# Building a graph aggregation's dense blocks: chunk order, table storage, and where the gathered steps stand

## What is computed

```python
def _graph_conv(x, W, edge_src, edge_dst, edge_weight, n_nodes):
    support = x @ W
    msg = support[edge_src] * edge_weight[:, None]
    return jax.ops.segment_sum(msg, edge_dst, num_segments=n_nodes)
...
h = _graph_conv(features, W1, edge_src, edge_dst, edge_weight, n)
out = _graph_conv(h, W2, edge_src, edge_dst, edge_weight, n)
...
xn = _layernorm(x, axis=-1)
x = x + _L0_gnn_ref(xn, ...) + _L0_mix_ref(xn[None], ...)[0]
x = x + _L0_ffn_ref(_layernorm(x, axis=-1)[None], ...)[0]
```

## Time and profile before

| | us |
|---|---|
| median of the three runs | 3638.55 |
| profiled execution, its own time | 3613.85 |
| its span | 3612.2 |
| TensorE busy, and its share of the span | 2916.3 (81%) |
| layer 1, unit 0 (76.2 to 149.6) | 73.4 |
| layer 1, units 1 to 26 (149.6 to 1512.2) | 1362.6 |
| all that follows, layer 2 first | 2100.0 |

### The profile page before, as it was taken

How to read it: one execution, slowest core, us unless ns; L and a number is a source line. 1 busy time by engine, 2 the same in 40 slices (tenths; PEclk the granted TensorE clock), 3 DMA queues, 4 the chain that set the end, 5 groups by cost and what they waited for, 6 DMA issues and landing times.

```text
span 3612.2 us, 49615 instructions
## 1 busy us (share of the span) xinstructions
PE 2916.3 (81%) x14732; PEld 2068.0 (57%) x14733; DVE 1420.1 (39%) x3945; ACT 1455.2 (40%) x3127; POOL 1844.7 (51%) x1924
## 2 busy tenths in 40 slices
PE   1799999899989999768988888888877648988930
PEld 0466556556656665546655666566546647777830
DVE  7544554554455446322222222222215541111157
ACT  4677776777777777300000000000004423333322
POOL 3555555545555555256666666666643651222235
PEclk9899999999999999979998999999988869999975
DMA  6344434434443443375555555555532334444454
GB/s 217 119 137 142 143 108 142 142 103 143 146 139 114 141 146 131 104 236 173 177 173 167 174 178 177 164 178 176 174 93 88 119 123 131 135 142 131 118 155 125
DMA packets 257759, 525.92 MB, mean 146 GB/s; under 512 B 47793, under 2 KB 144056, under 8 KB 257337
## 3 DMA queue, kind: packets, MB, share of 16 engines
q1 hardware_dynamic: 142492, 263.69, 22.4%
q0 software_dynamic: 84240, 228.40, 21.0%
q10 hardware_dynamic: 30832, 31.42, 2.7%
HBM read 387.33 MB, written 137.44 MB: 145 GB/s over the span
## 4 chain that ended last, share of the span: by engine, by line
PE 52%; issue 12%; DVE 11%; another core or an unknown queue 10%; ACT 6%; DMA 5%; SPq 3%; DVEq 1%; ACTq 1%; POOL 0%; POOLq 0%
PE bank L911 28%; PE bank L899 8%; PE sums L924 5%; DVE pa L1295 4%; DMA pa<-ys_d 4%; PE bank L1134 3%; PE bank L988 2%; PE bank L934 1%; ACT build L709 1%; ACT build L707 1%; PE sums L882 1%; ACT pa L833 1%; PE bank L943 1%; SPq L537 1%
## 5 line engine op out<-in xcount | busy, mean ns | idle before, releaser
L606 POOL DMA_INDIRECT pa<-xn_d,srcs x768 | 739.8, 963 | 667.4 <-PE sums L924 481.6
L606 POOL DMA_INDIRECT pa<-h_d,srcs x768 | 756.1, 985 | 398.2 <-issue 212.6
L911 PE MATMUL bank<-t1s,pa 128*128 128x256 f32 x2646 | 657.6, 398 | 100.0 <-issue 79.8
L899 PE MATMUL bank<-build 128*128 128x343 f32 x1620 | 559.9, 477 | 130.5 <-DVE build L1280 54.7
L1295 DVE TENSOR_TENSOR pa<-bank,pa 128x343 f32 x810 | 417.4, 515 | 603.8 <-ACT pa L714 462.8
L911 PE MATMUL bank<-t0s,pa 128*128 128x256 f32 x2646 | 612.5, 389 | 45.2 <-DVE pa L1295 37.4
L911 PEld LDWEIGHTS bank<-t1s,pa 128*128 128x128 f32 x2646 | 515.8, 199 | 231.5 <-issue 143.2
L911 PEld LDWEIGHTS bank<-t0s,pa 128*128 128x128 f32 x2646 | 504.7, 194 | 155.4 <-issue 86.2
L899 PEld LDWEIGHTS bank<-build 128*128 128x128 f32 x1620 | 279.8, 192 | 376.1 <-issue 298.1
L709 ACT ACTIVATE build<-build,ones 128x343 f32<-128x343 f32 x810 | 471.3, 582 | 26.3
L707 ACT ACTIVATE build<-build,l1tab 128x343 f32<-128x343 f32 x810 | 458.8, 566 | 37.3 <-issue 24.6
(11 more groups left out here) (247 smaller groups left out, 2565.9 us busy)
## 6 DMA issues: line engine op xcount, KB each, us to landing
slab_d<-pa SPq DMA_DIRECT2D x189, 448.0 KB
pa<-slab_d SPq DMA_DIRECT2D x189, 448.0 KB
pa<-in_w ACTq DMA_DIRECT2D x32, 512.0 KB, 4.0
pa<-in_w SPq DMA_DIRECT2D x32, 512.0 KB, 3.7
pa<-ys_d SPq DMA_DIRECT2D x109, 130.0 KB
pa<-eo_d SPq DMA_DIRECT2D x49, 256.0 KB, 3.2
pa<-xn_d,srcs POOLq DMA_INDIRECT x768
pa<-h_d,srcs POOLq DMA_INDIRECT x768
```

The costliest lines, as they stand in the source:

```text
L606: pool.indirect_dma_start(gath[g % RING * QT + j], None, table, bass.IndirectOffsetOnAxis(ap=srcs[:, n:n + 1], axis=0)).then_inc(s_g[g % R ...
L899: pe.matmul(bld[c % BLD][:, 0:WT], lohot[c % LR], mvs[c % MR], start=True, stop=True).then_inc(s_bmm, 1)
L911: ins = pe.matmul(app[:, 0:D], slab3[:, s, :], table[:, s * D:(s + 1) * D], start=s == 0, stop=s == T - 1)
```

## The change

1. Chunks of a unit are taken alternately from its two halves (0, 15, 1, 16, ...: `chunk_at`). Neighbours in this order touch columns that are at least 7 apart, so an add waits for the last but one (the last unit excepted). The start computes whether this holds for the data (`apart`) and otherwise turns to the loop for irregular rows.
2. `lo` and `nkey` (as `tab_d`) and `off` (as `off_d`) are computed in the scratch front of `t1s` and stored to DRAM. Two sets of small SBUF tables hold a unit each. SP reloads one set per unit with three DMAs, ahead of the unit's seven slab stores. POOL's last clearing of `t1s` covers 4824 columns where it had covered 2394, and also waits for the stores of the tables.
3. The memory that this frees goes to LR = 12 and MR = 18 buffers. 12 and 15 one-hots are written ahead during the apply (2 and 3 at each place).
4. All gathered steps of layer 1 stand in the build: after chunks 2, 6, 10, 14, 18, 22, 26 (and 28 in the units of eight).
5. DVE adds the dense product of the unit before at p = 0 and no longer after chunk 6, writes its placing one-hots at p = 3 and no longer after chunk 20, and reads the registers for the next unit right after a build's last add.

```diff
-LR = 10
-MR = 10
+LR = 12
+MR = 18
+EARLY_LO = 12
+EARLY_MV = 15
+TABS = 2
-CREDIT = 12
+CREDIT = 20
-EARLY = 2
...
-        SLOT1 = (("m", 4), ("m", 11), ("m", 18), ("m", 25), ("p", 0), ("p", 2), ("p", 4), ("p", 5))
+        SLOT1 = (("m", 2), ("m", 6), ("m", 10), ("m", 14), ("m", 18), ("m", 22), ("m", 26), ("m", 28))
...
+        def chunk_at(m):
+
+            return m // 2 + m % 2 * (KB // 2)
...
+            sp.wait_ge(s_tab, 1)
+            sp.dma_start(tab_d, tab).then_inc(s_tst, 16)
+            sp.dma_start(off_d, off[0:1, :]).then_inc(s_tst, 16)
+            sp.wait_ge(s_tst, 32)
+
+            def turn_tables(i):
+                b = i % TABS
+                sp.wait_ge(s_lo, (i - TABS) * KB + KB)
+                sp.wait_ge(s_mv, (i - TABS) * KB + KB)
+                c = i * KB
+                sp.dma_start(tabs[b][:, 0:2, :], tab_d.rearrange("p (k c) -> p k c", k=2)[:, :, c:c + KB]).then_inc(s_tl[b], 16)
+                sp.dma_start(tabs[b][:, 2, :], wt_t[:, C0 + c:C0 + c + KB]).then_inc(s_tl[b], 16)
+                sp.dma_start(offs[b][:], off_d[:, c:c + KB]).then_inc(s_tl[b], 16)
...
                 sp.wait_ge(s_bev, i * KB + KB + BLD)
+                if i + TABS < NU:
+                    turn_tables(i + TABS)
...
             pool.wait_ge(s_tab, 1)
-            pool.memset(t1s[:, 0:NCH + DC], 0.0).then_inc(s_t1z, 1)
+            pool.wait_ge(s_tst, 32)
+            pool.memset(t1s[:, 0:SCRATCH], 0.0).then_inc(s_t1z, 1)
...
-                        for m in range(p * EARLY, min(MR, (p + 1) * EARLY)):
-                            moving(i * KB + KB + m)
+                        for m in range(p * 3, min(EARLY_MV, (p + 1) * 3)):
+                            moving(i + 1, m)
                         blanks(i, p)
...
-                dve.wait_ge(s_bev, c + BLD)
-                part = slab3[:, :, bass.ds(at, W)]
+                dve.wait_ge(s_bev, c + BLD - (0 if i == NU - 1 else 1))
+                part = slab3[:, :, bass.ds(at[chunk_at(m)], W)]
...
-                    if m == 6 and i > 0:
+                if i < NU - 1:
+                    at = None
+                    at = offsets(i + 1)
+                for p in range(CT):
+                    if p == 0 and i > 0:
                         place_add(1, GU + i - 1, t1s)
-                    if m == 20:
+                    if p == 3:
                         dense_hots(i, 0)
```

More of the change, by code:

```diff
@@ L74 @@
 assert KV * KVT + 1 == T and KVT + 2 < NU
-assert KB % LR == 0 and KB % 5 == 0 and QK % HK == 0 and FG * P <= HB * HK * P
+assert KB % 2 == 0 and EARLY_LO <= LR and EARLY_MV <= MR and QK % HK == 0 and FG * P <= HB * HK * P
 class Links:
@@ L172, in gps_layer @@
         build = sb("build", [P, LR * P + MR * WT + WT])
-        l1tab = sb("l1tab", [P, 3 * DC])
+        tabs = [sb(f"tabs{b}", [P, 3, KB]) for b in range(TABS)]
+        offs = [sb(f"offs{b}", [1, KB], I32) for b in range(TABS)]
         srcs = sb("srcs", [P, C0], I32)
         dstf = sb("dstf", [P, C0])
-        wts = sb("wts", [P, NCH])
+        wts = sb("wts", [P, C0])
         mnmx = sb("mnmx", [MMP, MMC, 2], I32)
@@ L254, in gps_layer @@
         xT = build[:, 3584:3840].rearrange("p (a q) -> p a q", a=2)
-        r8 = l1tab[:, 1840:1856].rearrange("p (m h) -> p m h", m=2)
-        hsum = l1tab[:, 1856:1872]
+        after = build[:, 4024:5896]
+        r8 = after[:, 1840:1856].rearrange("p (m h) -> p m h", m=2)
+        hsum = after[:, 1856:1872]
         t1 = sq.rearrange("p (a n) -> p a n", a=2)
@@ L335, in gps_layer @@
         s_z = sem("s_z"); s_ap = sem("s_ap"); s_t1z = sem("s_t1z")
+        s_tst = sem("s_tst"); s_tl = [sem(f"s_tl{b}") for b in range(TABS)]
         s_obg = sem("s_obg"); s_hpg = sem("s_hpg"); s_plg = sem("s_plg"); s_pag = sem("s_pag")
@@ L735, in _ @@
             act.wait_ge(s_tab, 1)
-            for c in range(MR):
-                moving(c)
+            for m in range(EARLY_MV):
+                moving(0, m)
             for i in range(NU):
                 for m in range(KB):
-                    if m + MR < KB:
-                        moving(i * KB + m + MR)
+                    if m + EARLY_MV < KB:
+                        moving(i, m + EARLY_MV)
                     takes(steps_at(i, "m", m, 0), 0)
@@ L1238, in _ @@
             link(dve.tensor_copy(lo, src_i))
+            for b in range(TABS):
+                link(dve.tensor_copy(tabs[b][:, 0:2, :], tab.rearrange("p (k c) -> p k c", k=2)[:, :, b * KB:(b + 1) * KB]))
+                link(dve.tensor_copy(offs[b][:], off[0:1, b * KB:(b + 1) * KB]))
             link(dve.tensor_copy(t0_i[:], dk0[:]))
```

84 lines of the change are left out of this document (52 added, 32 removed).

## The result

The changed kernel took 3893.34 us (median of four runs, 3888.09 to 3903.08), the kernel before 3634.45 beside it: ratio 1.0716, 95% interval 1.0679 to 1.0753. I had forecast 3603 us and a range up to 3638. Its profiled execution has a span of 3889.5 us.

A forecast was written before the change was run, and what follows sets the result against it. Layer 1 was taken as bound by TensorE, leaving idle time and lowered clock to win. Units 1 to 26 -36 us, unit 0 +5, layer 1's end -4.5: -35.5 from 3638.55 gave 3603 us, range 3562 to 3638.

The forecast's parts named there:

- The step that failed: POOL's gathers in layer 1: seven steps take 35 us of a 50 us unit, so no wait was forecast.
- The last add but one: DVE's adds in units 1 to 26: waiting one add further back gains 0.65 us a unit, bounds 0 and 0.85.
- Rival B: DVE's adds don't get faster; 0.2 us a unit is left, total 3634 us; chance 0.16.
- All gathered steps in the build: TensorE's idle time before chunks in units 1 to 26 falls from 2.3 to 1.7 us: gain 0.6 a unit.
- heavy step: Gathered step, one in six, where DVE's one-hots and a `place_add` fall together; TensorE then waits 1.2 us.
- ScalarE and SP: Table loads delay slab stores and ScalarE's blanks, which have 0.6 us to spare: cost 0.15 us a unit, between 0 and 3.0.
- rival C: Table loads delay slab stores and ScalarE's chain of blanks, costing 3.0 us a unit; total 3677 us; chance 0.09.
- Clock: TensorE's clock in units 1 to 26 falls less often with less idle time: gain 0.3 us a unit, between 0 and 1.
- Unit 0 and the start: Start of layer 1 and its first unit: 5 us longer, between -10 and +15.
- start chain: Instructions ahead of unit 0: eleven more for the tables, 4 us, all on the path.
- My credit of 3 us: Unit 0 ends 73 us after the start chain's mark, where it ended 76 us after it.
- The end of layer 1: The loop for irregular rows no longer waits for gathers and starts with DVE's one-hots: 4.5 us gained.

The follow-up runs named there:

- late job: Kind of measuring job in which the unchanged kernel before takes 3620 to 3635 us; semaphore updates come late in its traces.
- prompt job: Kind of measuring job in which the unchanged kernel before takes 3420 to 3425 us; the changed kernel takes 3401 us there, ratio 0.9942.
- e13: The changed kernel as it is, measured again in a prompt job: 3401.19 us, ratio 0.9942.
- e10: The kernel before with rests (six POOL memsets after each gathered step of layer 1), in a prompt job: 3419.37 us, ratio 0.9990.
- e18: The changed kernel with the old places of the gathered steps and each add waiting for the one before, in a prompt job: 3391.23 us, ratio 0.9912.
- e16: The changed kernel with the gathered steps at their old places, no rests, in a prompt job: 3351.88 us, ratio 0.9791.
- e1: The changed kernel with the gathered steps at their old places, in a late job: 3587.45 us, ratio 0.9884.
- e2: The kernel before with only the new places of layer 1's gathered steps, in a late job: 3891.67 us, ratio 1.0719.
- e6: The changed kernel with layer 1 gathers fetching half of each row, as many descriptors, in a late job: 3937.41 us, ratio 1.0883.
- e5: The changed kernel with two POOL memsets after each gathered step of layer 1, in a late job: 3858.69 us, ratio 1.0643.
- e12: The changed kernel with four POOL memsets after each gathered step of layer 1, in a prompt job: 3404.3 us, ratio 0.9939.

## Why the prediction was wrong, step by step

**The step that failed** is POOL's: "No wait. POOL's idle time of 640.5 us is the cover". I asked only whether gathers would be ready in time. I didn't ask what a faster row of them does to others. The old places held most gathers apart by themselves, for each ring place fell free some us after the one before: behind unit 0, 140 of the 184 steps of the kernel before start 5.3 to 8 us after the step before, and 7 sooner. The new places leave POOL waiting through the apply and then let it run at 1.26 us a gather: 88 steps start within 5.3 us. In a late job TensorE's updates then come late, and units 1 to 26 take 1635.4 us where the same program takes 1313.2 in a prompt job and 1311.8 with rests in a late one. The trace of before had the sign of it, and I passed it by: unit 0, where 24 gathers stood in a row, had 18 us of idle time "whose cause I can't name". In e10, with rests and in a prompt job, that unit takes 55.3 us where it took 73.4. The other sign was the "remote" and "issue" waits of layer 2.

**The sum, term by term, where no update is late** (e13 against e10, 20.4 us between their spans): unit 0 and the start +14.6, units 1 to 26 -28.2, the rest -6.8. I had +5, -36 and -4.5. As e10 has rests and the kernel before has none, a few us of each can be theirs.

- *The last add but one*: 0.65 us a unit forecast, **1.5 measured** (e18 against e16), in late jobs 2.2 (56 over 26). The idle time before the apply fell to 1.0 us a unit (25.8 over 26), where I had 1.05. But the faster adds also help within the build, of which I had counted nothing here. Rival B is refuted: the adds do get faster. Late in a build of e18, with the old wait, they start 0.72 us apart, and in e13 three of them take 1.35 us together, 0.42 apart:

```profile
714.12 0.52 DVE L1349 TENSOR_TENSOR pa<-bank,pa 128x343 f32 x1 [0.20 <-DVE pa L1349]
714.84 0.52 DVE L1349 TENSOR_TENSOR pa<-bank,pa 128x343 f32 x1 [0.20 <-DVE pa L1349]
```

```profile
723.49 1.35 DVE L1349 TENSOR_TENSOR pa<-bank,pa 128x343 f32 x3
```

The Trainium skill ("VectorE: DVE Perf Modes", "The DRAIN you can't avoid") says of a chain of copies that the semaphore after each costs nothing extra. It also says that an operation which is not held starts earlier, which my prediction had left out. For these adds the traces show the second: waiting for the last add but one was worth 39 us.

- *All gathered steps in the build*: idle time before chunks 1.7 us a unit forecast, 1.56 measured (40.6 over 26). I had a heavy step cost 0.6 us a unit more with all steps in the build (1.4 against 0.8). The places themselves cost 0.2 to 0.5 a unit (above), so the size was about right; that it is the heavy steps was not tested by itself.
- *ScalarE and SP*: 0.15 us a unit forecast, **about 1.05 measured**. It is rival C's mechanism, blank for blank, at a smaller price than its 3.0. I had put 0.6 us of spare time against a delay of 1.3; the delay was 1.57, and the copy that TensorE waits for stood at the end of the chain. It cost 23 us more than I had, for the spare time was not there.
- *Clock*: 0.3 us a unit forecast. Granted 1.00 in the units of e13, 0.99 in e10's.
- *Unit 0 and the start*: +5 forecast (-10 to +15), +14.6 measured, +23.2 in the late job. The start chain's mark comes 2.8 us later (DVE at 76.06 in e13, 73.30 before) and so does the first chunk (79.05 and 76.29), where I had 4. The stores of the tables took 3.7 us from their issue (76.15) and not 6, so the first gather stands at 84.10 where it stood at 75.68, 8.4 us later and not 12. But 7 steps must pass in one build, 10.2 us of the 14.6 by e13 against e16:

```profile
79.81 4.12 POOL L630 MEMSET t1s<- 128x4824 f32 x1 [64.05 <-DMA off_d<-t1s]
84.10 1.17 POOL L639 DMA_INDIRECT pa<-xn_d,srcs  x1 [0.18 <-issue]
```

My credit of 3 us rested on unit 0 ending 76 us after the mark before, and that held the 18 us of idle time. Where late updates are absent, as in e10, the longer row of gathers is plain loss.

- *The end of layer 1*: -4.5 forecast. TensorE's first matmul of the loop for irregular rows came 12.5 us after the last unit (1512.2 to 1524.70), now 8.2 in e13 and 8.2 in the late job's profile (1808.2 to 1816.36): -4.3. It waits for DVE's one-hots, as forecast, and no longer for gathers:

```profile
1467.48 3.78 PE L1001 MATMUL sums<-pa,hots 128*128 128x256 f32 x8 [6.45 <-DVE hots L1427]
```

  For layer 2 and the rest I had 0. In the late profiles what follows layer 1 takes 2078 to 2101 us whatever the program, so the other 14 of the 18.7 us that the result was shorter there are no gain of the change.

So in a prompt job 20 of the forecast 35.5 us came, by gains that were larger (the adds, and the 29 us of e18) and a ScalarE chain and a start that were dearer than I had them. That the total comes within 16 us of the forecast there is in part luck: errors of both signs cancel. In the late kind of job, in which both the profile of before and the result were taken, all this is buried under 277 us.

## What to carry to other kernels

A queue that "has room" is not free to run faster: ask what paces it now, and what its row looks like once that is gone; waits put down to "remote" or "issue" on engines that are usually matched are the warning. Where an edit moves work only in order, try that order alone and the rest alone (e1 and e2) before any story about the parts. And run the kernel before in every job: a change that looked 7% slower was 0.6% faster in a later job, and only the pairs within a job told which part of that was the edit's.

## What was not expected of the hardware

In late jobs, TensorE's semaphore updates reach DVE and POOL some 4 us late and more while POOL (GpSimd) issues indirect gathers 1.26 or 1.43 us apart (DVE's longest wait on "remote" in units 1 to 26 is 7.2 us, and TensorE stands for 16.7 us without a releaser in the long row of unit 0). At 1.64 and 1.69 us apart the units of layer 1 lose nothing. Fewer bytes do not help (e6), nor does one short break per step (e5). The row of gathers is itself not slowed: 967 ns a gather in the late job, 970 in e13. In prompt jobs the same rows leave no idle time without a releaser before TensorE's matmuls of layer 1 (e13).

What makes a job late or prompt stays open: no experiment of mine could choose the kind. That half of the update records are missing in late jobs alone would fit a crowded path for event records, and in the burst at 823.35 us the updates of TensorE and the landings of DMAs follow one another within 0.3 us. Every run on record, also those that only give a time, lists its span and clock, so no run here was seen without such records, and whether updates come late without them is open. The Trainium skill ("NOTIFIC — the notification-queue block", "7.1 Overflow: three behaviours, one of which stalls the engine") tells of a queue of records that can stall the engine which writes them. No run here shows that this is what happened.

Whether the limit of the rate lies nearer 1.43 or 1.64 us is open too, for e12 met a prompt job.
